# Graph attention and mixture-of-experts kernel on one core: scaling a batch ahead of the next one's statistics, and loading rows one iteration sooner

## What is computed

```python
x = x + gnn(layernorm(x), edges, ...)
x = x + experts(layernorm(x), ...)

def gnn(x, ...):
    xn = layer_norm(x, ln1_g, ln1_b)          # node stage
    h = (xn @ W).reshape(N, 8, 32)            # node stage
    a_src = einsum(h, att_src); a_dst = einsum(h, att_dst)   # node stage
    e = leaky_relu(a_src[src] + a_dst[dst], 0.2)             # edge stage from here
    alpha = softmax of e over the edges with the same dst
    out = segment_sum(h[src] * alpha, dst) + xn @ W_res + bias
    out = layer_norm(out, ln2_g, ln2_b)
    return out + gelu(out @ ffn_w1 + ffn_b1) @ ffn_w2 + ffn_b2
```

## Time and profile before

| | us |
|---|---|
| median of 3 runs | 2410.7 (2405.38 to 2410.88) |
| the profiled execution, its own time | 2414.63 |
| its span in the profile | 2413.4 |
| PE busy | 2032.3 (84% of the span) |
| DVE busy | 1664.7 (69%) |
| ACT busy | 1446.1 (60%) |
| POOL busy | 1198.5 (50%) |
| mean granted PE clock, share of full speed | 0.846 |

### The profile page before, as it was taken

One profiled execution on the slowest core, in us unless ns is written; L12 is line 12 of the kernel. 1 busy time (PEld: TensorE's weight loads), 2 busy tenths in 40 slices (PEclk: granted clock), 3 DMA queues, 4 the chain that ended last, 5 costly groups with the idle time before them and its releaser, 6 DMA issues.

```text
span 2413.4 us, 50990 instructions
## 1 busy us (share of the span) xinstructions
PE 2032.3 (84%) x16714; PEld 1763.8 (73%) x16714; DVE 1664.7 (69%) x5180; ACT 1446.1 (60%) x3212; POOL 1198.5 (50%) x1155
## 2 busy tenths in 40 slices
PE   3737888888888888888775999999399999999998
PEld 2525666666666666666664888888399999999998
DVE  4518888888888888888898677776344444444443
ACT  1345566666666666666662677776366666666664
POOL 2147777777777777777760033334222222222223
PEclk8866777777777777777777999999699999999999
DMA  5666666666666666666663122222624245325322
GB/s 129 186 156 184 184 180 183 180 181 179 182 184 184 183 183 185 191 168 183 171 184 103 53 89 89 87 74 70 242 46 115 46 113 150 83 46 150 81 46 36
DMA packets 207788, 329.48 MB, mean 137 GB/s; under 512 B 43286, under 2 KB 147056, under 8 KB 202788
## 3 DMA queue, kind: packets, MB, share of 16 engines
q0 software_dynamic: 63840, 151.61, 26.6%
q1 hardware_dynamic: 143108, 173.52, 22.6%
q10 hardware_dynamic: 576, 1.09, 0.2%
HBM read 431.90 MB, written 95.53 MB: 219 GB/s over the span
## 4 chain that ended last, share of the span: by engine, by line
PE 56%; DVE 15%; issue 10%; ACT 10%; DMA 4%; POOL 2%; DVEq 1%; SPq 1%; ACTq 0%; POOLq 0%
PE bank L920 17%; PE bank L1096 10%; PE bank L1097 10%; PE bank L1098 10%; DVE edge_mem L986 6%; ACT edge_mem L819 3%; PE bank L890 2%; DMA edge_mem<-in_x 2%; ACT layer_hid L1191 1%; PE bank L506 1%; DVE win_mem L1012 1%; POOL edge_mem L729 1%; ACT piece_hi L711 1%; ACT layer_mem L1190 1%; PE bank L1807 1%
## 5 line engine op out<-in xcount | busy, mean ns | idle before, releaser
L729 POOL DMA_INDIRECT edge_mem<-node_table,src_col x880 | 839.1, 953 | 291.7 <-issue 263.2
L920 PE MATMUL bank<-edge_mem 128*128 128x264 f32 x1760 | 536.2, 471 | 50.8 <-DVE edge_mem L986 41.5
L920 PEld LDWEIGHTS bank<-edge_mem 128*128 128x128 f32 x1760 | 408.1, 238 | 160.7 <-DVE edge_mem L986 45.2
L1096 PE MATMUL bank<-expert_rounded 128*128 128x256 f32 x1792 | 512.8, 286 | 0.0
L1098 PE MATMUL bank<-expert_rounded 128*128 128x256 f32 x1792 | 508.3, 284 | 0.0
L1097 PE MATMUL bank<-expert_rounded 128*128 128x256 f32 x1792 | 508.1, 284 | 0.0
L1793 POOL DMA_INDIRECT out<-expert_mem,slot_tok x112 | 192.3, 1717 | 507.8 <-DVE expert_mem L1731 487.8
L1092 DVE TENSOR_TENSOR expert_rounded<-expert_mem,expert_rounded 128x512 fp32r<-128x512 f32 x280 | 194.1, 693 | 261.6 <-ACT expert_rounded L1780 196.5
L1780 ACT ACTIVATE expert_mem<-bank,par 128x256 f32<-128x256 f32 x448 | 227.3, 507 | 231.0 <-PE bank L1098 231.0
L1096 PEld LDWEIGHTS bank<-expert_rounded 128*128 128x128 f32 x1792 | 345.3, 193 | 0.0
L1097 PEld LDWEIGHTS bank<-expert_rounded 128*128 128x128 f32 x1792 | 345.1, 193 | 0.0
(11 more groups left out here) (230 smaller groups left out, 3787.7 us busy)
## 6 DMA issues: line engine op xcount, KB each, us to landing
expert_rounded<-split_w SPq DMA_DIRECT2D x224, 1024.0 KB
split_w<-piece_hi SPq DMA_DIRECT2D x72, 256.0 KB
split_w<-piece_lo SPq DMA_DIRECT2D x72, 256.0 KB
piece_full<-in_L_ffn_W SPq DMA_DIRECT2D x64, 256.0 KB
expert_mem<-expert_rows SPq DMA_DIRECT2D x56, 265.0 KB, 3.2
edge_mem<-node_table,src_col POOLq DMA_INDIRECT x880
node_table<-win_mem SPq DMA_DIRECT2D x12, 544.0 KB, 3.3
xn_in<-turned SPq DMA_DIRECT2D x49, 128.0 KB
```

Of the source, the lines that this page charges most:

```text
L729: pool.indirect_dma_start(gath[g % NGB][:, t, :], None, node_table, bass.IndirectOffsetOnAxis(ap=src_col[:, k, t % 2:t % 2 + 1], axis=0)). ...
L920: ins = pe.matmul(bank[5 + at % 3][:, 0:AGG], onehot[g % 2][:, 2 * k + j, :], gath[g % NGB][:, 2 * k + j, 0:AGG], start=(j == 0), stop=(j ...
L1096: pe.matmul(out_ap, s_hi, m_lo, start=start, stop=False)
```

## The change

SP issues the load of batch 2 ahead of its loop, and in iteration i the load of batch i + 2 behind the turned stores of batch i - 1 and ahead of the table store of batch i - 2. Before, it issued the load of batch i + 1 first in iteration i. DVE scales batch i - 1 before it takes the statistics of batch i, instead of after.

```diff
--- before.py
+++ after.py
@@ -331,11 +331,12 @@
             load_x(1)
+            load_x(2)
             for i in range(1, NB + 2):
-                if i + 1 < NB:
-                    load_x(i + 1)
                 if i <= NB:
                     store_turned(i - 1)
+                if i + 2 < NB:
+                    load_x(i + 2)
                 if i >= 2:
                     store_table(i - 2)
                 prep_sp(i)
@@ -416,10 +417,10 @@
                     dve.memset(buf[:, n - 1, :], 0.0).then_inc(tail_cleared, 1)
+                if i <= NB:
+                    node_norm(i - 1)
                 if i < NB:
                     node_stats(i)
-                if i <= NB:
-                    node_norm(i - 1)
                 if i == 1:
                     attention_columns()
```

## The result

The changed kernel takes 2386.1 us (median of 4, 2378.7 to 2388.7) where the kernel before takes 2410.6 beside it (median of 4, 2405.4 to 2410.9). The ratio is 0.9893, 95% interval 0.9874 to 0.9911: 25.8 us less, between 21.5 and 30.4. The profiled execution took 2378.7 us with a span of 2377.5, the low end of these runs.

What follows compares the result with a forecast made beforehand. The edge stage's gathers keep their pace and start when the node stage ends. The list brought the first gather 32 us sooner, less 2 for cold PE starts: 30 saved, 2381 us against 2410.7, range 2372 to 2395.

Steps and rivals of the forecast that it cites:

- rival A: SP's queue, node stage: load 6 stuck behind batch 2's stores and step_win, 6 us later; 2391 to 2397; chance 0.2.
- B: Rival on SP's queue: load 5 slips past the slow step_win store, larger saving, 2373 us; chance 0.09.
- C: Rival: edge stage held by its own constants or weight pieces, giving most back, 2408 or so; chance 0.05.
- D: Rival: DVE becomes serial, 22 us added over 13 batches if loads land no sooner, 2433 us; chance 0.04.
- The list of times: Node stage, step by step across SP, DVE and PE, up to the first gather at 112.1 us against 144.1.
- Load 6: SP's load of batch 6: inherits load 5's old place plus 1.7 us, landing at 53.7, just in time.
- The clock: PE, node stage: 2 us taken off for two low-clock starts; otherwise products of 3.83 us from about 60 us.
- The roots: POOL's root between a batch's statistics and scaling, DVE idle where no preparation covers it: counted 1.2 us with semaphores.
- The tail wait: Load 12 on SP waits for DVE's clearing of the tail buffer, about 93.3; covered by 1.5 us of PE work.
- The edge stage: POOL's 880 gathers keep their own pace; moving the first gather moves the end by about as much.
- the 19.57 us hole: DVE's idle time before batch 4 lands at 50.66, part of the node stage's largest hole; forecast gone.
- part 2: SP's reordering: load 4 issued at about 27.6 instead of 35.29, ahead of step_win, landing at 33.2.

Runs made afterwards that it cites:

- run 5: The kernel before, unedited and profiled once more, on a chip where the gathers of either kernel stretch; 3360.3 us.
- run 1: The kernel before with only DVE's order changed, scaling ahead of the next statistics, SP's queue as before; 2384.5 us, ratio 0.9927.
- run 2: The changed kernel with DVE's order undone, so only SP's order differs from the kernel before; 2388.5 us, ratio 0.9945.
- run 9: The kernel before with step_win stored as 128 rows of 16 bytes, read back by two transfers; 2406.4 us against 2406.6, ratio 0.9998.
- run 10: The kernel before with DVE's new order alone and step_win in rows of 16 bytes; 2382.0 us, ratio 0.9891.
- run 11: The kernel before with SP's new order alone and step_win in rows of 16 bytes; 2383.9 us, ratio 0.9908.
- run 3: The changed kernel with step_win stored as 128 rows of 16 bytes, read back by two transfers; 2372.3 us, ratio 0.9880.
- run 12: The changed kernel with step_win in rows of 16 bytes and DVE's window words behind the last scaling; 2370.7 us, ratio 0.9845.
- run 6: The changed kernel, unedited, once more, on the same chip as run 5; 3330.6 us, ratio 0.9917.

## Why the prediction was right

**The time.** 2381 was forecast, 2386.1 measured; 30 us saved against 24.4 by the medians, 25.8 by the ratio and 27.0 by the first gather. The forecast's band was 26 to 34 us and rival A's 14 to 25, so the measured saving lies at the border of the two, and the time range holds both. A's own sum, 2391 to 2397, was not reached; B (2373), C (2408) and D (2433) did not happen. All of it was reckoned from one profile of the kernel before, whose gathers start at 144.1. In run 5 they start at 138.3, and against that one the change saves 21.0 us. How much of the near hit is owed to that one profile the runs do not settle.

**The list of times**, step by step, forecast and profile:

| step | forecast | measured |
|---|---|---|
| scaling of batch 1 starts | 22.5 | 22.58 |
| load 4 issued | 27.6 | 27.78 |
| step_win issued | 31.6 | 32.01 |
| batch 4 taken by DVE | 33.3 | 32.82 |
| load 5 there | 49.1 | 49.74 |
| load 6 there | 53.7 | 56.97 |
| window words start | 77.7 | 82.03 |
| load 12 issued | 93.3 | 97.58 |
| first gather | 112.1, about 114 with two cold starts | 117.1 |

Up to load 5 every entry is within 0.7 us. **Load 6** is the term that was mis-sized, by 3.3 us. I gave it load 5's old place plus one more pair of stores. In fact SP was held twice before it had issued it, 7.98 us in the turned stores of batch 3 and 4.18 in load 6 itself. That is the first half of rival A with load 6 late by 3.3 us instead of 6. The wait that A named happened too: ACT stood 7.4 us, until the stores of batch 2 had landed. But it lay beside DVE's wait for load 5. **The clock** was the other term: I took off 2 us for two places, and the products of batches 4, 5 and 8 took 5.50, 5.54 and 5.60 us in place of 3.83. The last two lie on the chain, 1.7 and 1.8 us. So the window words start 4.3 us late (3.3 of load 6 and 1.7 of product(5), less 0.7 that other steps were shorter), product(8) adds 1.8, the rest gives 1.1 back, and the first gather is 5.0 after the listed 112.1.

The forecast of the clock failed also as a sign: products of 3.83 from about 60 us on was wrong for those of batches 5 and 8. How long step_win took to land, the profile of the changed kernel does not give; it was 10.8 us in runs 1 and 2 and 10.5 in run 5.

**The roots** cost about what was said: six waits, 7.4 us in all. The wait is 1.12 and 1.16 us where only the root stands between statistics and scaling, less where preparation covers it, and 3.1 once, behind POOL's gathers of edge rows. That last one was not in the list; batch 5 was late anyway. **The tail wait** was covered: batch 12 was scaled by 104.0, turn(12) ran at 108.0. **The edge stage** kept its pace: 1109 to 1113 us from first to last gather in all ten profiles on the faster chips, whatever the order.

**What was right in the number and wrong in the reason.** The prediction called the 19.57 us hole the largest and said of part 2 that "the 19.57 us are gone". The sum did not rest on it, since it carried the whole list to the end, but the emphasis was wrong. Run 1 keeps 13.90 us of the hole and still has its first gather at 118.3; run 9 nearly halves the hole and takes the same time as the kernel before. The waits for loads fell by 28.7 us: batches 4 and 5 together by 10.3 (the wait moved from one to the other and shrank), batch 6 by 6.4, batch 12 by 6.7, batches 8 and 10 by 4.1, the first two by 1.2. So the hole is about a third, and the rest are later waits in which scaling, load and table store held each other. Either part alone breaks that ring, by runs 1, 2, 10 and 11; that every one of the 28.7 us lay on the chain was not shown. Had I split the gain between the parts I would have been wrong, as the expectations of runs 1 and 2 were.

**The 2 KB store.** The Trainium skill (DMA: Bandwidth & Descriptors, Anatomy of one DMA) has a fit for the POOL path, about 2.0 us plus the bytes over 436 GB/s, which would give this store 2 us (an estimate by that page). The measurement decides against it here: the store landed in 10.5 to 11.8 us as 4-byte pieces (the kernel before, runs 1, 2 and 5) and in 4.2 to 5.7 us as 16-byte rows (runs 3 and 9 to 12).

## What to carry to other kernels

A long wait in a timeline is not what its removal is worth: here, as long as the ring of waits stood, shortening the longest one left the time as it was, and cutting the ring at either of two places brought most of the gain. So carry the times of every engine through to the end of the stage instead of subtracting the hole. And look at tiny transfers in a busy queue: with 2 KB in pieces of 4 bytes the changed kernel's first gather came 8.7 us later than with pieces of 16. Last, one profile of each kernel is not enough for a difference of a few microseconds: the node stage of the kernel before varied by 5.8 us.

## What the runs showed of the hardware

- 512 pieces of 4 bytes kept the DMA engines at a busy share of 0.98 while 31 GB/s moved; as 128 pieces of 16 bytes, 358 GB/s moved in the same stretch. Issued from ACT's queue they still held SP's issues (8.11 us).
- An issue can hold SP: 7.98 us for a pair of stores that took 0.91 elsewhere, while step_win's pieces were under way. Everything behind it on SP stood still. What the issue waits for is not shown.
- A GpSimd root took 1.24 us beside DVE's scalings and 1.01 to 1.05 in ten of the twelve places of the new order (the other two: 1.11 and 1.30, beside the attention columns and the window words). In some of the ten DVE was busy as well, with column copies or the clearing of a buffer, so a busy DVE alone does not make a root slower.
- On one chip the gathers of both kernels stretched over 2011 to 2012 us in place of 1109 to 1113, with a node stage within what is seen elsewhere. In run 6 POOL waited 924.3 us for PE between its gathers (7.7 in the first profile of that kernel), and DVE 937.8 us at L1034, which by the code waits among others for gathered rows. That points at the gathered rows' landing; the cause is open.
